# Cross attention in a decoder layer: the row sums of seven batches go through DRAM to 128 rows of 32, are inverted there and come back spread

## The chip, the cores and the metric

One core of a Trainium2 chip runs the whole kernel. The metric is the device time of one execution in microseconds; the median of several runs counts. Five engines work side by side, each through a queue of its own in program order: TensorE (PE in the profile, its weight loads PEld), VectorE (DVE), ScalarE (ACT), GpSimd (POOL) and SyncE (SP, which only issues transfers here). They wait for one another by semaphores.

## What is computed

The reference is a decoder layer over 8 batches of 256 tokens of width 128: self attention with a position bias, cross attention to a context of 1601 rows a batch, a second self attention, a feed-forward block and a mixture of experts. The change lies in the cross attention alone, which is, cut to what matters:

```python
q = _split_heads(x @ qw + qb)          # 16 heads of 8
k = _split_heads(ctx @ kw + kb)
v = _split_heads(ctx @ vw + vb)
scores = jnp.einsum('bqhd,bkhd->bhqk', q, k) / np.sqrt(D // H) + mask
probs = jax.nn.softmax(scores, axis=-1)
out = jnp.einsum('bhqk,bkhd->bqhd', probs, v)
```

The kernel takes the exponentials of the scores less their row maximum, multiplies them by the values with a column of ones beside them, so that every head's product brings its row sum along, and divides at the end, once a batch.

## The kernel before

`phase_cross` (L1244) is the stage in question; it runs from about 210 to 901 us. Its work is cut into 64 units, a unit g being one pair of heads p = 0 to 7 of one batch b. `cross_steps` (L1220) goes through the steps -2 to 64 and hands every engine the same plan, `cross_plan(p)` (L1181), of which each engine runs the kinds that it has an action for. So all engines' queues have the same order, written out by hand. A step of the plan has 13 rounds j, and in them:

- `s`, 13 score tiles of the unit, three rounds ahead: two matmuls on TensorE each (L1360), one exponential on ScalarE (L1478) into one of 8 buffers PT;
- `g`, 16 grains of the unit two steps ahead: a matmul of the scores laid the other way (L1342) into one of 4 banks, and a reduction to the row maximum on VectorE (L1558); `neg` (L1565) joins and negates them;
- `split` (L1635), four small operations on GpSimd that split the negated maxima into three bfloat16 parts, at the very end of a step for the unit two steps ahead; `m` in round 7 of the next step turns them on TensorE (L1391), and ScalarE puts them beside the queries (L1486), where the unit's scores wait for them;
- `v`, three bursts of products with the values (L1380) in rounds 3, 7 and 12, which add up in the bank PO; `o` at the end of the step copies it to a slot of OT (L1494, ScalarE), of which there are ten;
- in rounds 5 and 10 the preparation of the next batch: `T` (p = 0, 1) turns its context (L1405), `K` (p = 2, 3) makes its keys, which GpSimd splits (L1633 to L1661), `V` (p = 4, 5) makes its values (L1583, VectorE).

`c` divides. In round 1 of p = 0 of the next batch TensorE waits for the last copy to OT and runs `head_sums` (L237): 16 float32 matmuls with the selector SEL over the batch's eight slots of OT, of which eight put the values of all 16 heads on 128 rows of 256 queries and eight put each head's row sum on its eight rows (`kind` 0 and 1). Each matmul shows as two records in the trace. VectorE then takes the reciprocal of the sums, 128 x 256 (L1571), and multiplies (L1573) into CAT. The score tiles, `m`, `c`, `T`, `K` and `V` take turns on three banks (`cross_ring` L1237, `take_bank` L1309), so a bank that is held long stops TensorE three turns later.

SyncE meanwhile stores the parts of the keys (L1712) and loads them, eight pairs a batch (L1721, L1722), and the queries every second batch. GpSimd issues no transfer in this stage. The self-attention stages already have the row sums go to DRAM and back, through SyncE (L904 to L927, L1119, L1124).

## Time and profile before

| | us |
|---|---|
| median of 3 runs | 1294.16 |
| lowest and highest run | 1292.65, 1294.98 |
| the profiled execution | 1292.28 |
| its span, first to last instruction | 1290.3 |
| mean granted TensorE clock | 0.92 of full speed |

The rows below are of that execution. A row of the timeline gives the start, the length (with xN, of N instructions merged), the engine, the line, the operation with out<-in, and in brackets how long the engine was idle before and what ended that. A row of windows gives a stretch, its length, and each engine's busy time with the count of instructions; behind them stand the granted clock, the share of the DMA engines' time and GB/s. A busy matmul is not TensorE at its peak, since matmuls are pipelined.

### The profile page before, as it was taken

To read this page: it belongs to the slowest core of one execution; us is meant where nothing else is said; L and a number is where in the kernel's file an instruction comes from. 1 tells how busy PE (TensorE), PEld (TensorE's weight loads), DVE (VectorE), ACT (ScalarE), POOL (GpSimd) and SP (SyncE) were. 2 spreads that over 40 slices of the span, in tenths; PEclk is the share of its full clock that TensorE was granted. 3 is DMA by queue.
4 is the path that set the end of the run, shared out by engine and by line. 5 is a ranking of instruction groups with operands and counts; after the bars stand their busy time and mean duration, and the time that the engine had idled before them with its cause. 6 is when DMAs were issued, how large, how long until landed. Compare 5 with 4: busy or idle time off the path is not lost. (4 is left out here: it accounts for less than half of the span.)

```text
span 1290.3 us, 32652 instructions
## 1 busy us (share of the span) xinstructions
PE 1077.4 (83%) x11660; PEld 576.5 (45%) x11660; DVE 995.1 (77%) x2779; ACT 860.7 (67%) x1764; POOL 406.4 (31%) x832
## 2 busy tenths in 40 slices
PE   5779995699999999999999999997667878539993
PEld 2334443244444444444444444443433445428883
DVE  7458766588889888898888988992777968766664
ACT  3468883087888878877788787785357965425553
POOL 3211213214150230502305023011442515755662
PEclk8689998689999999999999999998878999759997
DMA  6934015523223132231322303100373012301113
GB/s 164 219 70 96 24 29 139 139 65 78 61 55 98 55 79 62 62 95 51 79 62 60 95 27 79 53 5 3 103 148 63 14 46 94 106 13 40 46 48 115
DMA packets 82974, 94.84 MB, mean 73 GB/s; under 512 B 12775, under 2 KB 69039, under 8 KB 82816
## 3 DMA queue, kind: packets, MB, share of 16 engines
q1 hardware_dynamic: 78720, 86.46, 26.7%
q0 software_dynamic: 2496, 5.12, 1.5%
q8 instruction: 96, 1.57, 0.5%
q10 hardware_dynamic: 1600, 1.18, 0.4%
q14 instruction: 62, 0.51, 0.1%
HBM read 66.47 MB, written 27.48 MB: 73 GB/s over the span
## 5 line engine op out<-in xcount | busy, mean ns | idle before, releaser
L1558 DVE TENSOR_REDUCE MG<-bank 128x1 f32<-128x401 f32 (+1 forms) x1024 | 515.4, 566 | 75.2 <-PE bank L1342 73.3
L1478 ACT ACTIVATE PT<-bank 128x512 f32<-128x512 f32 (+1 forms) x624 | 334.7, 597 | 64.2 <-PE bank L1360 63.6
L1360 PE MATMUL bank<-QP,KP 54*128 54x256 bf16 (+1 forms) x1664 | 252.5, 274 | 16.2 <-DVE CAT L1573 4.1
L1342 PE MATMUL bank<-KP,QP 54*128 54x401 bf16 (+1 forms) x1024 | 237.1, 344 | 14.7 <-DMA KP<-ctx_k_parts 9.5
L1380 PE MATMUL bank<-PT,VP 128*9 128x256 f32 (+1 forms) x2688 | 198.2, 368 | 0.8 <-ACT XT L1478 0.8
L1633 POOL TENSOR_TENSOR MP<-MN,ZERO 128x4 bf16<-128x4 f32 x128 | 26.4, 206 | 440.9 <-DVE MN L1565 435.9
L1360 PEld LDWEIGHTS bank<-QP,KP 54*128 54x128 bf16 (+1 forms) x1664 | 110.6, 96 | 108.1 <-ACT PT L1478 24.4
L1342 PEld LDWEIGHTS bank<-KP,QP 54*128 54x128 bf16 x1024 | 75.5, 94 | 125.0 <-DVE MG L1558 93.2
L1004 PE MATMUL bank<-QP,KP 51*128 51x256 bf16 x512 | 97.9, 285 | 39.1 <-DMA QP<-q_parts 12.5
L1478 ACT ACTIVATE XT<-bank 128x512 f32<-128x512 f32 (+1 forms) x208 | 116.2, 599 | 20.3 <-PE bank L1360 19.9
L971 PE MATMUL bank<-KP,QP 51*128 51x256 bf16 x512 | 100.7, 294 | 3.9 <-DVE MG L1099 1.0
L1380 PEld LDWEIGHTS bank<-PT,VP 128*9 128x9 f32 (+1 forms) x2688 | 76.1, 90 | 57.9 <-issue 20.9
L1099 DVE CUSTOM_DVE_ANT_0 JUNK<-bank,UQ 128x256 bf16<-128x256 f32 x256 | 92.4, 420 | 6.7 <-PE bank L971 6.6
L1061 ACT ACTIVATE XT<-bank 128x512 f32<-128x512 f32 x128 | 74.5, 602 | 27.3 <-PE bank L1004 26.6
L1380 PE MATMUL bank<-XT,VP 128*9 128x256 f32 (+1 forms) x896 | 91.9, 369 | 0.0
L1105 DVE TENSOR_REDUCE MN<-bank 128x2 f32<-128x512 f32 x128 | 81.1, 683 | 3.6 <-PE bank L971 1.4
L1150 POOL TENSOR_TENSOR MP<-MN,ZERO 128x8 bf16<-128x8 f32 x128 | 26.4, 206 | 182.1 <-DVE MN L1112 114.1
L1004 PEld LDWEIGHTS bank<-QP,KP 51*128 51x128 bf16 x512 | 33.3, 96 | 110.3 <-issue 68.3
L935 ACT COPY QP<-bank 3x512 bf16<-3x512 bf16 x96 | 55.1, 574 | 36.2 <-PE bank L1038 35.7
L2163 PE MATMUL bank<-WUP,XP 128*128 x234 | 64.1, 409 | 2.4 <-DVE XP L2332 2.4
L1486 ACT COPY QP<-bank 3x256 bf16<-3x256 bf16 x128 | 45.3, 354 | 26.4 <-DMA q_parts<-PT 25.7
L1633 POOL TENSOR_TENSOR KPARTS<-XT,ZERO 128x401 bf16<-128x401 f32 (+1 forms) x56 | 47.6, 851 | 36.7 <-ACT XT L1506 34.5
(283 smaller groups left out, 1870.7 us busy)
## 6 DMA issues: line engine op xcount, KB each, us to landing
KP<-ctx_k_parts SPq DMA_DIRECT2D x128, 100.1 KB
ctx_k_parts<-KPARTS SPq DMA_DIRECT2D x16, 600.4 KB, 5.3
KP<-ctx_k_parts SPq DMA_DIRECT2D x128, 59.4 KB
CN<-in_ctx SPq DMA_DIRECT2D x8, 768.0 KB
RAW<-in_w_gate_up SPq DMA_DIRECT2D x8, 512.0 KB, 3.7
QP<-q_parts SPq DMA_DIRECT2D x20, 192.0 KB
ctx_k_parts<-KPARTS SPq DMA_DIRECT2D x16, 200.1 KB, 5.4
UQ<-bias_table SPq DMA_DIRECT2D x4, 768.0 KB, 8.3
```

The source lines that it names most:

```text
L971: last = nc.tensor.matmul(bank[:, S * qt:S * (qt + 1)], k.QP[rows, p, a:a + 128], k.KP[rows, p, b * S:(b + 1) * S], start=True, stop=True)
L1004: last = nc.tensor.matmul(bank[:, S * t:S * (t + 1)], k.KP[half(s), p, a:a + 128], k.QP[half(s), p, b * S:(b + 1) * S], start=not bias, st ...
L1061: nc.scalar.activation(PT[n % 8], SCORE[n % 3][:, :], ACT.Exp).then_inc(exp_done, 1)
L1099: last = nc.vector.tensor_tensor_reduce(out=JUNK[:, 2 * (n % 2) + q, :], in0=bank[:, S * q:S * (q + 1)], in1=k.UQ[:, 2 * p + s, 128 * q:12 ...
L1105: nc.vector.tensor_reduce(MN[:, u % 3, j, s, :], bank[:, :].rearrange("p (q n) -> p q n", q=QT), AX.X, ALU.max, negate=True).then_inc(grai ...
L1342: nc.tensor.matmul(GRAIN[n % NG][:, 0:w], k.QP[half, p, b * S + 128 * qt:b * S + 128 * (qt + 1)], k.KP[half, p, a:a + w], start=True, stop ...
L1360: return nc.tensor.matmul(bank[0:rows[t], S * at:S * (at + 1)], k.KP[half, p, 128 * t:128 * t + rows[t]], k.QP[half, p, b * S:(b + 1) * S] ...
L1380: last = nc.tensor.matmul(k.PO[32 * c:32 * c + HD + 1, q:q + w], VP[b % 2][0:rows[t], t, 2 * p + s, :], PT[(T * g + n) % NP][0:rows[t], S ...
L1478: nc.scalar.activation(PT[n % NP][0:rows[t], :], bank_of("s", g, t)[0:rows[t], :], ACT.Exp).then_inc(exp_done, 1)
L1558: nc.vector.tensor_reduce(MG[:, g % 4, 2 * s + qt, chunk:chunk + 1], GRAIN[n % NG][:, 0:w], AX.X, ALU.max).then_inc(m_read, 1)
L1633: return nc.gpsimd.tensor_tensor(out, x, ZERO[:, :].broadcast_to(list(x.shape)), ALU.add)
L2163: last = nc.tensor.matmul(bank[j % 2], XP[:, j % 2, a, :], WUP[:, bass.ds(e, 1), b, n0:n0 + FF].rearrange("p a n -> p (a n)"), start=(n == ...
```

## The change

For the batches 0 to 6 the row sums no longer go through TensorE. GpSimd, at the end of every step (`o`), waits for the copy to OT and sends the four rows that hold the sums to DRAM (`take_sums`). At p = 0 of the next batch it waits for all eight and loads the sums as 128 rows of 32, in two halves (`spread_sums`, `x`). At p = 1 VectorE adds the halves and takes the reciprocal of 128 x 32 (`reciprocals`, `r`), and GpSimd sends that to DRAM and loads it back spread over 128 rows of 256 (`return_reciprocals`). At p = 2 TensorE selects the values alone, eight matmuls (`batch_values`, `c`), and VectorE multiplies (`scale`). ScalarE's copy to a slot of OT waits for the slot's transfer too. The last batch is divided as before (`e`).

```diff
--- before.py
+++ after.py
@@ -162,6 +162,7 @@
     k.dYS = dram("expert_rows", [2 * TOK + 128 * SLOT_TILES, D], F32)
     k.dSums = dram("head_sums", [H, S], F32)
     k.dRec = dram("head_reciprocals", [H, S], F32)
+    k.dHalves = dram("half_sums", [PAIRS, 4, S], F32)
     k.dMask = dram("mask_parts", [3, B * NCTX], BF16)
 
 
@@ -234,9 +235,9 @@
     return divmod(g, PAIRS)
 
 
-def head_sums(k, bank, slot_of, b):
-
-    for kind in range(2):
+def head_sums(k, bank, slot_of, b, kinds=(0, 1)):
+
+    for kind in kinds:
         for parity in range(2):
             for j in range(4):
                 last = k.nc.tensor.matmul(bank[32 * j:32 * j + 32, S * kind:S * (kind + 1)], k.SEL[:, kind, parity, :],
@@ -1194,8 +1195,10 @@
             plan.append(("h", T - 1, t // T))
         if j in (5, 10) and rounds:
             plan.append(rounds[j // 10])
-        if j == 1 and p == 0:
-            plan.append(("c", 0, 0))
+        if j == 1 and p < 3:
+            plan.append((("e", "r", "c")[p], 0, 0))
+            if p == 0:
+                plan.append(("x", 0, 0))
         if j in bursts:
             if bursts[j] == 1:
                 plan.append(("m", 0, 1))
@@ -1227,8 +1230,11 @@
             if what in ("T", "K", "V"):
                 if 0 <= b < LAST_BATCH:
                     actions[what](b + 1, i)
-            elif what == "c":
-                if b > 0:
+            elif what in "rcx":
+                if 0 < b < B:
+                    actions[what](b - 1, i)
+            elif what == "e":
+                if b == B:
                     actions[what](b - 1, i)
             elif 0 <= step + ahead < B * PAIRS:
                 actions[what](step + ahead, i)
@@ -1237,7 +1243,7 @@
 def cross_ring():
 
     turns = [(what, 0, i) for what in "TKV" for i in range(4)]
-    cross_steps({what: lambda unit, i, what=what: turns.append((what, unit, i)) for what in "smcTKV"})
+    cross_steps({what: lambda unit, i, what=what: turns.append((what, unit, i)) for what in "smceTKV"})
     return turns
 
 
@@ -1275,6 +1281,7 @@
         MN = k.sb("MN", [128, 4, 4], stack=st)
         MP = k.sb("MP", [128, 4, 4, 3], BF16, stack=st)
         REC = k.sb("REC", [128, S], stack=st)
+        SUMS = k.sb("SUMS", [128, 4, SEGMENT], stack=st)
         ZERO = k.sb("ZERO", [128, 1], stack=st)
         CN = k.sb("CN", [128, T, D], stack=st)
         CT = k.sb("CT", [128, T * 128], stack=st)
@@ -1289,6 +1296,8 @@
         neg_ready, max_split, m_turned, m_rows = sem("neg_ready"), sem("max_split"), sem("m_turned"), sem("m_rows")
         s_ready, exp_done, pv_done = sem("s_ready"), sem("exp_done"), sem("pv_done")
         o_read, sums_turned, rec_done, sums_done = sem("o_read"), sem("sums_turned"), sem("rec_done"), sem("sums_done")
+        sums_out, sums_in, sums_added = sem("sums_out"), sem("sums_in"), sem("sums_added")
+        compact_done, rec_out, rec_in = sem("compact_done"), sem("rec_out"), sem("rec_in")
         qk_in = [sem(f"qk_in{c}") for c in range(4)]
         vp_set, zero_made, psum_cleared = sem("vp_set"), sem("zero_made"), sem("psum_cleared")
         ctx_in, ctx_turned, ctx_t_taken = sem("ctx_in"), sem("ctx_turned"), sem("ctx_t_taken")
@@ -1315,7 +1324,7 @@
                         pe.wait_ge(exp_done, T * a + j + 1)
                     elif old == "m":
                         pe.wait_ge(m_rows, a + 1)
-                    elif old == "c":
+                    elif old in "ce":
                         pe.wait_ge(sums_done, a + 1)
                     elif old == "T":
                         pe.wait_ge(ctx_t_taken, 4 * a + j + 1)
@@ -1392,9 +1401,13 @@
                                                k.IDB[:, :])
                 last.then_inc(m_turned, 1)
 
-            def batch_sums(b, i):
+            def batch_values(b, i):
                 pe.wait_ge(o_read, PAIRS * (b + 1))
-                head_sums(k, take_bank("c", b, i), lambda g: OT[:, g % NO, :], b).then_inc(sums_turned, 1)
+                head_sums(k, take_bank("c", b, i), lambda g: OT[:, g % NO, :], b, (0,)).then_inc(sums_turned, 1)
+
+            def last_values(b, i):
+                pe.wait_ge(o_read, PAIRS * (b + 1))
+                head_sums(k, take_bank("e", b, i), lambda g: OT[:, g % NO, :], b).then_inc(sums_turned, 1)
 
             def turn_context(b, i):
                 if i == 0:
@@ -1463,8 +1476,8 @@
                 make_queries(g)
             for i in range(4):
                 make_values(0, i)
-            cross_steps({"s": scores, "h": last_tile, "g": grain, "v": values, "m": max_rows, "c": batch_sums,
-                         "T": turn_context, "K": make_keys, "V": make_values})
+            cross_steps({"s": scores, "h": last_tile, "g": grain, "v": values, "m": max_rows, "c": batch_values,
+                         "e": last_values, "T": turn_context, "K": make_keys, "V": make_values})
 
         @block.scalar
         def _(act):
@@ -1491,6 +1504,7 @@
                 act.wait_ge(pv_done, NV * (g + 1))
                 if g >= NO:
                     act.wait_ge(sums_turned, (g - NO) // PAIRS + 1)
+                    act.wait_ge(sums_out, 16 * PAIRS * ((g - NO) // PAIRS + 1))
                 nc.scalar.copy(OT[:, g % NO, :], k.PO[:, 0:S]).then_inc(o_read, 1)
 
             def take_turned(b, i):
@@ -1565,11 +1579,26 @@
                 nc.vector.tensor_reduce(MN[:, g % 4, :], MG[:, g % 4, :, :], AX.X, ALU.max,
                                         negate=True).then_inc(neg_ready, 1)
 
-            def divide(b, i):
-                bank = bank_of("c", b, i)
+            def reciprocals(b, i):
+                v.wait_ge(sums_in, 32 * (b + 1))
+                nc.vector.tensor_tensor(SUMS[:, 2, :], SUMS[:, 0, :], SUMS[:, 1, :], ALU.add).then_inc(sums_added, 1)
+                v.wait_ge(sums_added, b + 1)
+                if b > 0:
+                    v.wait_ge(rec_out, 16 * b)
+                nc.vector.reciprocal(SUMS[:, 3, :], SUMS[:, 2, :]).then_inc(compact_done, 1)
+
+            def scale(b, i):
+                v.wait_ge(rec_in, 16 * (b + 1))
                 v.wait_ge(sums_turned, b + 1)
+                nc.vector.tensor_tensor(k.CAT[:, b * S:(b + 1) * S], bank_of("c", b, i)[:, 0:S], REC[:, :],
+                                        ALU.mult).then_inc(sums_done, 1)
+
+            def divide_last(b, i):
+                bank = bank_of("e", b, i)
+                v.wait_ge(sums_turned, b + 1)
+                v.wait_ge(sums_done, b)
                 nc.vector.reciprocal(REC[:, :], bank[:, S:2 * S]).then_inc(rec_done, 1)
-                v.wait_ge(rec_done, b + 1)
+                v.wait_ge(rec_done, 1)
                 nc.vector.tensor_tensor(k.CAT[:, b * S:(b + 1) * S], bank[:, 0:S], REC[:, :],
                                         ALU.mult).then_inc(sums_done, 1)
 
@@ -1622,7 +1651,7 @@
             v.wait_ge(late_in, 48)
             for i in range(4):
                 take_values(0, i)
-            cross_steps({"g": maxima, "neg": negate, "c": divide, "V": take_values})
+            cross_steps({"g": maxima, "neg": negate, "r": reciprocals, "c": scale, "e": divide_last, "V": take_values})
 
         @block.gpsimd
         def _(pl):
@@ -1681,7 +1710,37 @@
             split_first_keys(3)
             split_queries(2)
             split_queries(3)
-            cross_steps({"split": split_maxima, "K": split_keys})
+            def take_sums(g, i):
+                b, p = batch_of(g)
+                if b == LAST_BATCH:
+                    return
+                pl.wait_ge(o_read, g + 1)
+                if p == 0 and b > 0:
+                    pl.wait_ge(sums_in, 32 * b)
+                nc.gpsimd.dma_start(k.dHalves.ap()[p], OT[HD:128:32, g % NO, :]).then_inc(sums_out, 16)
+
+            def spread_sums(b, i):
+                pl.wait_ge(sums_out, 16 * PAIRS * (b + 1))
+                if b > 0:
+                    pl.wait_ge(compact_done, b)
+                for half in range(2):
+                    src = bass.AP(tensor=k.dHalves.ap().tensor, offset=2 * S * half,
+                                  ap=[[4 * S, PAIRS], [SEGMENT, 2 * S // SEGMENT], [1, SEGMENT]])
+                    nc.gpsimd.dma_start(SUMS[:, half, :], src).then_inc(sums_in, 16)
+
+            def return_reciprocals(b, i):
+                pl.wait_ge(compact_done, b + 1)
+                if b > 0:
+                    pl.wait_ge(rec_in, 16 * b)
+                nc.gpsimd.dma_start(compact(k.dRec), SUMS[:, 3, :]).then_inc(rec_out, 16)
+                pl.wait_ge(rec_out, 16 * (b + 1))
+                if b > 0:
+                    pl.wait_ge(sums_done, b)
+                src = bass.AP(tensor=k.dRec.ap().tensor, offset=0, ap=[[S, H], [0, HD], [1, S]])
+                nc.gpsimd.dma_start(REC[:, :], src).then_inc(rec_in, 16)
+
+            cross_steps({"split": split_maxima, "K": split_keys, "o": take_sums, "x": spread_sums,
+                         "r": return_reciprocals})
             pl.wait_ge(late_in, 48)
             pl.wait_ge(y_turned, 4)
             for g in range(4):
```

## Rows read from the trace of the kernel before

**Rows 1.** The page's part 1: busy time, share of the span, instructions.

```profile
PE 1077.4 (83%) x11660; PEld 576.5 (45%) x11660; DVE 995.1 (77%) x2779; ACT 860.7 (67%) x1764; POOL 406.4 (31%) x832
```

**Rows 2.** Windows, copy L1494 to copy: stretch, length, PE, PEld, DVE, ACT, POOL busy.

```profile
420.65:432.83 12.18, 11.18 (x145) 5.33 (x143) 10.57 (x21) 8.82 (x19) 0.82 (x4) 1.00 0.16 50
432.83:442.32 9.49, 9.12 (x110) 4.37 (x108) 8.02 (x17) 8.10 (x18) 0.81 (x4) 1.00 0.13 42
442.32:452.31 9.99, 9.55 (x109) 4.24 (x107) 8.51 (x18) 8.71 (x18) 5.61 (x10) 1.00 0.24 66
...
483.11:491.90 8.79, 8.24 (x105) 3.80 (x103) 8.12 (x18) 7.51 (x17) 0.82 (x4) 1.00 0.20 59
...
822.15:833.49 11.34, 10.50 (x137) 4.64 (x135) 10.22 (x20) 7.75 (x16) 0.81 (x4) 1.00 0.17 51
833.49:842.28 8.79, 8.24 (x105) 3.77 (x103) 8.14 (x18) 7.52 (x17) 0.81 (x4) 1.00 0.08 28
```

**Rows 3.** Timeline at the division of the second batch, p = 0.

```profile
420.65 0.37 ACT L1494 COPY OT<-bank 128x256 f32<-128x256 f32 x1 [0.51 <-PE bank L1380]
...
420.89 0.17 DVE L1565 TENSOR_REDUCE MN<-MG 128x4 f32<-128x16 f32 x1
...
421.05 1.06 DVE L1558 TENSOR_REDUCE MG<-bank 128x1 f32<-128x401 f32 x2
...
421.08 1.93 PE L242 MATMUL bank<-OT,SEL 128*32 128x256 f32 x32
...
422.95 0.35 PE L1342 MATMUL bank<-KP,QP 54*128 54x401 bf16 x2
...
423.08 1.76 DVE L1571 RECIPROCAL REC<-bank 128x256 f32<-128x256 f32 x1 [0.97 <-PE bank L242]
...
423.54 0.60 ACT L1478 ACTIVATE PT<-bank 128x512 f32<-128x512 f32 x1 [1.51 <-PE bank L1360]
...
424.87 0.42 DVE L1573 TENSOR_TENSOR CAT<-bank,REC 128x256 f32<-128x256 f32 x1
...
425.36 0.39 PE L1360 MATMUL bank<-QP,KP 54*128 54x256 bf16 x2 [0.58 <-DVE CAT L1573]
```

**Rows 4.** Timeline of a plain step, from 833.49 us.

```profile
833.89 2.02 DVE L1558 TENSOR_REDUCE MG<-bank 128x1 f32<-128x401 f32 x4
...
834.43 0.11 PEld L1360 LDWEIGHTS bank<-QP,KP 54*128 54x128 bf16 x2 [0.41 <-ACT PT L1478]
...
836.12 2.50 DVE L1558 TENSOR_REDUCE MG<-bank 128x1 f32<-128x401 f32 x5 [0.21 <-PE bank L1342]
```

**Rows 5.** One line's instructions: durations in ns, minimum, median, maximum.

```profile
L1119 DVE RECIPROCAL SUMS<-SUMS x14: 341/348/353, 95.7 to 1050.8; 128x32 f32<-128x32 f32 x14
```

**Rows 6.** GpSimd's own transfers, in the expert stage: durations, landings, one timeline row.

```profile
L2396 POOL DMA_INDIRECT XG<-expert_tokens,G_ROW x39: 952/977/1223, 1150.7 to 1258.5; - x39
...
DMA to landing us min/median/max: 2.4/2.7/3.6
...
1181.44 0.98 POOL L2396 DMA_INDIRECT XG<-expert_tokens,G_ROW  x1 [0.30 <-issue]
```

**Rows 7.** Timeline: last operation of a split on POOL, and L1391 after it.

```profile
413.20 0.21 POOL L1646 TENSOR_TENSOR MP<-MN,MP 128x4 bf16<-128x4 f32 x1
...
415.94 0.23 PE L1391 MATMUL bank<-IDB,MP 128*3 128x128 bf16 x2 [0.19 <-ACT PT L1478]
...
455.52 0.21 POOL L1646 TENSOR_TENSOR MP<-MN,MP 128x4 bf16<-128x4 f32 x1
...
456.94 0.23 PE L1391 MATMUL bank<-IDB,MP 128*3 128x128 bf16 x2 [0.26 <-ACT XT L1506]
...
465.48 0.21 POOL L1646 TENSOR_TENSOR MP<-MN,MP 128x4 bf16<-128x4 f32 x1
...
467.45 0.22 PE L1391 MATMUL bank<-IDB,MP 128*3 128x128 bf16 x2 [0.58 <-DVE VP L1583]
```

**Rows 8.** SyncE's queue: one line's issues in ns; landings of L927.

```profile
L1721 SPq DMA_DIRECT2D KP<-ctx_k_parts x128: 302/1973/2654, 236.4 to 827.2; - x128
...
DMA to landing us min/median/max: 2.3/2.4/4.4
```

## The prediction

> **What bounds the kernel now.** I read the busy time first: TensorE leads with 83% of the span, VectorE follows with 77% [rows 1]. That is an average over stages, so the second view was the cross-attention loop cut into its steps, from one copy of L1494 to the next [rows 2]. A step is one pair of heads of one batch, numbered p = 0 to 7 in a batch. A step without extra work (p = 6) takes 8.79 us, with TensorE busy for 8.24, VectorE for 8.12 and ScalarE for 7.51 of them: no engine has more than a few tenths of a microsecond to spare, and the three wait for each other in turn. Work put into a step therefore lengthens it, and the way to price the change is to compare steps. In the last batch nothing but the division stands between p = 0 (11.34 us) and the plain step after it (8.79 us): the present division costs 2.55 us a batch. The granted clock is 1.00 in all of these steps (the 2.4 GHz level), so no part of the sum is the clock's.
>
> The third view is the timeline at that place [rows 3]. TensorE spends from 421.08 to 422.95 us, 1.87 us, on the 16 selection matmuls (32 records). VectorE, done with two reductions at 422.11, waits until 423.08, divides (1.76 us) and multiplies (0.42 us). TensorE then waits 0.58 us for the bank of the product, and ScalarE is left without scores for 1.51 us.
>
> The fourth view is the same place in a plain step [rows 4]: TensorE waits 0.41 us for an exponential before the seventh score tile, and VectorE waits 0.21 us after its fourth reduction. These two gaps can swallow a small insert.
>
> **The change part by part.** *Removed from p = 0, seven times.* In the last batch it is worth 2.55 us by the subtraction above. In the six others p = 0 also turns two tiles of context; without the division it cannot be expected below p = 1 (9.49 us), which turns a full group and a short one, so at most 12.18 - 9.49 = 2.69 us goes. If p = 1's surplus of 0.70 us were 1.25 groups, a full one would cost 0.56, p = 0 would stay at 8.79 + 1.12 = 9.91, and 2.27 us would go. I take 2.55, since one price for the division then explains both kinds of p = 0. Seven times 2.55 is 17.85 us; the ends are 6 x 2.27 + 2.55 = 16.2 and 6 x 2.69 + 2.55 = 18.7.
>
> *Added to p = 2: eight matmuls and the multiplication.* Half of the 1.87 us is 0.93 us on TensorE. They sit ahead of the 0.41 us wait for the exponential, which goes on meanwhile, so 0.52 us remains. VectorE's 0.42 us multiplication follows its two reductions (about 1.06 us) and ends before TensorE's next grains are there; the bank is back before the third ring turn asks for it, so the 0.58 us wait goes too. The data of the wait on `o_read` have been there for two steps. Cost 7 x 0.52 = 3.6 us. Ends: 0.4 a batch (a little more absorbed), and half of today's 2.55, that is 1.28, if the insert costs in proportion: 2.8 and 9.0 us.
>
> *Added to p = 1: an addition and a reciprocal of 128 x 32.* The reciprocal of that shape takes 0.34 us in the self-attention stage; for the addition the nearest row is the 128 x 16 reduction, 0.17 us [rows 3, 5]. Together with the handover about 0.5 us on VectorE, of which the 0.21 us wait after the fourth reduction covers a part: 0.29 us a batch, 2.0 us in all. Ends 0 and 0.55: 0 and 3.9 us. The addition alone has bounds of nothing and 0.34 us, the reciprocal of its own size; I take the reduction's, the nearer in work.
>
> *GpSimd's queue.* In each of 56 steps a transfer of four rows of 1 KB now stands ahead of the four small operations that split the maxima, and it waits for the copy L1494. That copy ends at 421.02, the negated maxima are ready at 421.06 [rows 3], so the wait adds nothing; the issue does. No plain transfer is issued by GpSimd in this trace. Its indirect ones hold it 0.98 us, and 0.30 us passes to the next [rows 6]: 1.28 us, which I take, since that is its own queue. The lower bound is nothing (issued while it idles), the upper the longest issue of SyncE's loads of keys, 2.65 us [rows 8]. Behind it wait the split, then TensorE's turning of the maxima (L1391), then the scores of the next pair. The time from the end of the split to L1391 [rows 7] is 415.94 - 413.41 = 2.53 us in a plain step, 456.94 - 455.73 = 1.21 us in p = 3 and 467.45 - 465.69 = 1.76 us in p = 4, because GpSimd is still splitting keys at the ends of p = 2 and p = 3. So 1.28 us is hidden everywhere but in p = 3, where 0.07 us, with the signal some 0.15 us, is left: 7 x 0.15 = 1.0 us.
>
> *The chain of transfers.* The copy L1494 of p = 7 starts at 420.65 and ends at 421.02 [rows 3]. The row transfer issued then lands about 2.7 us later (the indirect median, [rows 6]), at 423.7; two spreading transfers are issued at 423.7 and 425.0 and land by 427.7. The addition on VectorE comes after the first two reductions of p = 1, 1.4 us behind the next copy (833.49 to 834.9 in [rows 2, 4]), at 420.65 + 9.63 + 1.4 = 431.7: 4.0 us to spare. From there 0.5 for addition and reciprocal, 2.7 for the way out and 2.7 for the way back give 437.6; the multiplication in p = 2 asks one step later, at 431.7 + 9.78 = 441.5: 3.9 us to spare. Even with 4.4 us for each landing, the longest of the same broadcast on SyncE's queue [rows 8], the addition's inputs land at 431.1 and the multiplication's at 441.0, just in time. I cost the waits at nothing; if the cover is gone, each microsecond late is a microsecond on VectorE in seven batches, 7 us. ScalarE's new wait, for the rows to have left their slot, is for transfers two steps old. `take_sums` of p = 0 also waits for the spread rows (427.7), three microseconds before its turn. The six semaphores and the unchanged last batch cost nothing.
>
> **The sum.** -17.85 + 3.6 + 2.0 + 1.0 = -11.2 us. The profiled execution took 1292.28 us (span 1290.3 us) and would come to 1281.1; the median of the runs stands 1.88 us above it, and by the same difference comes to 1283.0 us. The best ends together give -18.7 + 2.8 = -15.9 us (1278.3), the worst with GpSimd's 1.28 us -16.2 + 9.0 + 3.9 + 1.0 = -2.3 us (1291.9).
>
> **Rivals.** *The insert keeps its price.* What costs in p = 0 may be the interruption itself. For it: the 2.55 us are more than TensorE's 1.87. Against it: 0.58 us of them is the wait for the product's bank [rows 3], which goes. It gives -17.85 + 9.0 + 3.9 + 1.0 = -4.0 us, 1290.2 us.
>
> *The rows arrive late.* The transfers become the bound: VectorE waits at the addition or the multiplication. The addition is late once a landing takes more than (431.7 - 421.0 - 1.3) / 2 = 4.7 us, the multiplication beyond (441.5 - 432.2) / 2 = 4.65 us. At 5.1 us each the two waits are 0.8 + 0.9 = 1.7 us a batch, 11.9 us in all, and nothing of the gain is left: 1294.9 us. Against it stand medians of 2.4 to 2.7 us.
>
> *GpSimd is held, and the maxima come late.* This one ends slower, in the split queue at the head of p = 3 and p = 4. With an issue of x us these steps wait (x - 1.21) + (x - 1.76); without the 1.0 us of the sum -12.2 us has to be eaten, 1.74 us a batch, so it decides from x = 2.36 us. At SyncE's 2.65 us it is 2.33 us a batch, and the 16 plain steps p = 6 and p = 7 add 0.12 each: 7 x 2.33 + 16 x 0.12 = 18.2 us, so 1294.2 - 12.2 + 18.2 = 1300.2 us. For it: SyncE does take that long beside the loads of keys. Against it: GpSimd's own rows keep within 1.22 us.
>
> The Trainium skill, page "DMA: Bandwidth & Descriptors", section "Issuing engine by pattern", gives plain loads and stores to SyncE and only indirect ones to GpSimd, which speaks against this change; its page "SBUF — State Buffer", section "Who interferes with whom", says how this rival could come about: a transfer from GpSimd's queue cannot get its descriptors while VectorE runs an operation in a two-port mode. The same section exempts reductions, which are most of VectorE's work in this loop. By that rule GpSimd is not held, and no row here shows a plain GpSimd transfer beside reductions, so the rival keeps the smaller chance.
>
> *It doesn't do what it says* would show as unchanged steps; the work moved is visible in the code, and I give it nothing of its own.
>
> **How the numbers follow.** The forecast (a gain of 6 to 16 us) has 0.66, the insert that keeps its price 0.16, late rows 0.08, GpSimd held 0.10. A difference of 0.2% (2.6 us) is what a measurement of this kernel can tell from none. The first two cases are faster but for the far end of the second, and a little of the late rows: 0.83. Same is 0.08, from late rows and that end, slower 0.09, nearly all GpSimd's. The range, 1278 to 1292 us, holds the forecast with its bounds and the second case; both slow cases are left out, some 0.15.
>
> **What would show it.** Steps p = 0 near 9.63, p = 1 near 9.8, p = 2 near 10.5 and p = 3 near 10.15 us, with p = 4 to 7 as now; 16 records of L242 in p = 2; no VectorE wait at the new lines; GpSimd's transfers at about 1.0 us each. I am wrong if L1391 waits for GpSimd, if the addition waits for a transfer, or if p = 2 grows by more than 1 us.

## The result, and the profile after

| | before | after |
|---|---|---|
| median, us | 1294.57 (4 runs) | 1316.77 (4 runs) |
| lowest and highest run | 1292.65, 1295.32 | 1312.73, 1317.65 |
| profiled execution, its span | 1292.28, 1290.3 | 1317.65, 1315.4 |
| first copy L1494 / L1508 to the last in the loop | 272.80 to 894.17: 621.37 | 273.97 to 915.75: 641.78 |
| mean granted clock | 0.920 | 0.909 |

The ratio is 1.017 (95% interval 1.0149 to 1.0190): slower by 22 us, where 11 us less was forecast and the range ended at 1292. In the loop 20.4 us were lost. Line numbers moved: the copy to OT is L1508 now, the reduction L1572 (L1558), the score tiles L1369 (L1360), the selection L243 (L242), `m` L1400 (L1391). New are L1584 (addition), L1588 (reciprocal of 128 x 32), L1593 (product), and GpSimd's transfers L1720 (rows out), L1729 (rows spread), L1735 (reciprocals out) and L1740 (reciprocals back).

The page's busy times of the changed kernel:

```profile
PE 1086.7 (83%) x11548; PEld 579.4 (44%) x11548; DVE 985.1 (75%) x2786; ACT 861.7 (66%) x1764; POOL 455.2 (35%) x916
```

Beside [rows 1], VectorE has 10 us less work, as intended, and TensorE shows 9 us more although 112 records of it are gone: a first sign of a lower clock. Next the windows of the changed kernel, batch 2, from copy to copy (p = 0, 1, 2, 3 and 6), then p = 2 alone in three pieces; columns as in [rows 2]:

```profile
426.46:436.09 9.63, 9.27 (x113) 4.50 (x111) 8.47 (x19) 8.47 (x18) 2.66 (x7) 1.00 0.19 58
436.09:445.59 9.50, 9.13 (x110) 4.47 (x108) 8.42 (x19) 8.12 (x19) 2.56 (x7) 1.00 0.16 51
445.59:460.65 15.06, 12.32 (x125) 5.03 (x123) 8.83 (x19) 9.06 (x18) 6.21 (x11) 0.89 0.19 53
460.65:470.64 9.99, 9.55 (x109) 4.24 (x107) 8.34 (x17) 8.71 (x18) 8.52 (x14) 1.00 0.01 3
491.44:500.22 8.78, 8.22 (x105) 3.83 (x105) 8.11 (x18) 7.51 (x16) 1.40 (x5) 1.00 0.23 69
...
445.59:449.00 3.41, 3.19 (x46) 1.26 (x42) 1.23 (x3) 2.46 (x5) 1.41 (x5) 1.00 0.80 222
449.00:452.40 3.40, 0.94 (x6) 0.38 (x6) 1.51 (x4) 0.60 (x1) 0.00 (x0) 1.00 0.05 13
452.40:455.90 3.50, 3.50 (x25) 1.51 (x28) 2.37 (x5) 2.29 (x5) 1.21 (x2) 0.52 0.00 0
```

p = 0 fell from 12.18 us [rows 2] to 9.63, the number of the forecast. p = 1 and p = 3 are as before. The whole loss of this batch is in p = 2: 15.06 us where some 10.5 was forecast. Its middle 3.4 us have TensorE busy for 0.94, and in the 3.5 us after that its granted clock is 0.52, the 1.2 GHz level nearly throughout. Over the batches, p = 2 took 14.52, 15.06, 17.55, 16.62, 17.60, 11.39 and, in the last, 10.46 us; p = 1 took 12.16 in batch 1, where the granted clock fell too, and 9.5 to 10.2 after. The waits of the changed kernel (280 to 930 us: engine, line, what it waited for, us in total, times, longest) name what ends last:

```profile
DVE CAT L1593 <- DMA REC<-head_reciprocals: 25.7, 7, 5.7
...
DVE SUMS L1584 <- DMA SUMS<-half_sums: 4.6, 6, 1.5
...
POOL REC L1740 <- DMA head_reciprocals<-SUMS: 34.2, 7, 5.7
POOL half_sums L1720 <- DMA SUMS<-half_sums: 30.8, 6, 6.1
...
PE bank L1369 <- DVE CAT L1593: 16.8, 6, 4.4
```

VectorE waits at the product for the reciprocals to come back, in all seven batches (3.35, 3.85, 5.67, 4.14, 5.43, 1.41, 1.88 us), and TensorE behind it for the product's bank. One whole chain, batch 2, in the timeline of the changed kernel (POOL, DVE, SP, PE; columns as in [rows 3]):

```profile
427.12 0.58 POOL L1720 DMA_DIRECT2D half_sums<-OT  x1 [7.12 <-ACT OT L1508]
...
432.19 1.25 POOL L1729 DMA_DIRECT2D SUMS<-half_sums  x2 [3.41 <-DMA half_sums<-OT]
438.15 0.57 POOL L1720 DMA_DIRECT2D half_sums<-OT  x1 [4.71 <-DMA SUMS<-half_sums]
...
440.09 0.61 POOL L1735 DMA_DIRECT2D head_reciprocals<-SUMS  x1 [0.29 <-issue]
444.97 0.55 POOL L1740 DMA_DIRECT2D REC<-head_reciprocals  x1 [4.27 <-DMA head_reciprocals<-SUMS]
...
437.64 0.19 DVE L1584 TENSOR_TENSOR SUMS<-SUMS 128x32 f32<-128x32 f32 x1
437.86 0.35 DVE L1588 RECIPROCAL SUMS<-SUMS 128x32 f32<-128x32 f32 x1
...
450.88 0.42 DVE L1593 TENSOR_TENSOR CAT<-bank,REC 128x256 f32<-128x256 f32 x1 [3.85 <-DMA REC<-head_reciprocals]
...
443.27 0.40 SPq L1758 DMA_DIRECT2D CN<-in_ctx  x1
...
451.37 0.39 PE L1369 MATMUL bank<-QP,KP 54*128 54x256 bf16 x2 [2.59 <-DVE CAT L1593]
```

From the addition (437.64) to the product (450.88) 13.24 us pass; the forecast had 5.9. The product was asked for at 447.03, 9.4 us after the addition. The 7.3 us too many are 1.9 in which GpSimd holds the reciprocals back (it waited with p = 0's rows for the spread rows until 438.15, then did the split), 2.2 on the way out (440.09 to 444.97 is 4.9, not 2.7) and 3.2 on the way back (444.97 to 450.88 is 5.9, not 2.7). All seven, in ns and us, from the views of the three lines of the changed kernel:

```profile
L1729 POOL DMA_DIRECT2D SUMS<-half_sums x14: 612/628/637, 347.5 to 850.1; - x14
...
DMA to landing us min/median/max: 2.3/3.8/6.1
...
L1735 POOL DMA_DIRECT2D head_reciprocals<-SUMS x7: 589/601/623, 356.5 to 855.8; - x7
...
DMA to landing us min/median/max: 4.6/4.8/6.0
...
L1740 POOL DMA_DIRECT2D REC<-head_reciprocals x7: 548/548/551, 362.5 to 860.7; - x7
...
DMA to landing us min/median/max: 3.2/5.9/6.3
```

The issues are short, 0.55 to 0.63 us at the medians: GpSimd is not held. It is the landing that is long, the time from the issue until the last part of the transfer has arrived. Why, the packet records of the changed kernel show, here those of the last batch (start of the first packet to end of the last, count):

```text
reciprocals out, 1024 B   857.00-857.21: 15 packets    859.75-859.80: 1 packet
reciprocals back, 4096 B  861.95-862.47: 30 packets    864.68-865.01: 2 packets
SyncE's keys, 3202 B      855.10-864.68: 73 packets (of a longer stream, cut at 855), median 131 ns
```

Of 16 equal shares fifteen are there 1.4 to 1.8 us after the start of the issue (855.83 and 860.69), and the last comes some 2.5 us later. The last two packets of the way back start at 864.68, when the stream of key rows ends. That stream is 73 x 131 ns = 9.56 us of packets in 9.58 us: one after the other, as from one DMA engine, long after SyncE's last issue at 850.8. The late share of the way out runs in the one pause of that stream (859.76 to 859.80 us), with 37 of its packets still to come. So a late share does not wait until the stream is over: in both transfers here it waits for about 20 rows of keys, 2.6 and 2.4 us. The stream is the load of 19 rows (L1722 before, L1781 now): 59.4 KB, 19 packets of 131 ns, 2.5 us for each of two per pair of heads.

The Trainium skill, page "DMA: Bandwidth & Descriptors", section "Why a DMA increments its semaphore by 16 and not by 1", says that the transfer's slowest dimension decides over how many engines it is spread (the largest count up to 16 that divides it), and that it counts as landed only when the last of them has finished. By that rule 19 rows go through a single engine, and the packets above agree: 131 ns apart, none side by side.

### The profile page after: what moved, and what is told of

It is laid out like the page before. It is cut to its first block and busy times, and to the rows that moved or that the text cites. A ratio compares the mean times of both kernels' runs of the same rounds, so it can differ in the third digit from the quotient of the medians.

```text
span 1315.4 us, 32557 instructions
## 1 busy us (share of the span) xinstructions
PE 1086.7 (83%) x11548; PEld 579.4 (44%) x11548; DVE 985.1 (75%) x2786; ACT 861.7 (66%) x1764; POOL 455.2 (35%) x916
## 5 line engine op out<-in xcount | busy, mean ns | idle before, releaser
L1572 DVE TENSOR_REDUCE MG<-bank 128x1 f32<-128x401 f32 (+1 forms) x1024 | 514.7, 566 | 81.7 <-PE bank L1351 79.8
L1369 PE MATMUL bank<-QP,KP 54*128 54x256 bf16 (+1 forms) x1664 | 256.8, 277 | 29.0 <-DVE CAT L1593 16.8
L1351 PE MATMUL bank<-KP,QP 54*128 54x401 bf16 (+1 forms) x1024 | 240.2, 347 | 17.2 <-DMA KP<-ctx_k_parts 9.4
L1389 PE MATMUL bank<-PT,VP 128*9 128x256 f32 (+1 forms) x2688 | 200.9, 372 | 0.8 <-ACT XT L1491 0.8
L1369 PEld LDWEIGHTS bank<-QP,KP 54*128 54x128 bf16 (+1 forms) x1664 | 112.4, 97 | 121.8 <-ACT PT L1491 24.5
L1720 POOL DMA_DIRECT2D half_sums<-OT x56 | 32.9, 587 | 262.0 <-ACT OT L1508 231.2
## 6 DMA issues: line engine op xcount, KB each, us to landing
KP<-ctx_k_parts SPq DMA_DIRECT2D x128, 59.4 KB
```

Of the source, the lines that this page charges most:

```text
L1351: nc.tensor.matmul(GRAIN[n % NG][:, 0:w], k.QP[half, p, b * S + 128 * qt:b * S + 128 * (qt + 1)], k.KP[half, p, a:a + w], start=True, stop ...
L1369: return nc.tensor.matmul(bank[0:rows[t], S * at:S * (at + 1)], k.KP[half, p, 128 * t:128 * t + rows[t]], k.QP[half, p, b * S:(b + 1) * S] ...
L1389: last = nc.tensor.matmul(k.PO[32 * c:32 * c + HD + 1, q:q + w], VP[b % 2][0:rows[t], t, 2 * p + s, :], PT[(T * g + n) % NP][0:rows[t], S ...
L1572: nc.vector.tensor_reduce(MG[:, g % 4, 2 * s + qt, chunk:chunk + 1], GRAIN[n % NG][:, 0:w], AX.X, ALU.max).then_inc(m_read, 1)
```

## The experiments

**Theory A**: the 19-row loads keep one DMA engine busy, and every transfer that passes over all 16 waits for it. The rivals: GpSimd's queue itself is slow (theory B in the expectations), or its many small transfers disturb the loop; the chain is too long wherever it runs. **Theory C** came later, from the context load at 443.27 above.

**The 19 rows cut into 16 and 3**, in the changed kernel (LOADS counts three loads accordingly):

```diff
-                    sp.dma_start(k.KP[r + 4 * HD:r + 6 * HD + 3, p, 0:N],
-                                 dC[b, s, 2 * HD:4 * HD + 3, p, :]).then_inc(kp_in[p], 16)
+                    sp.dma_start(k.KP[r + 4 * HD:r + 6 * HD, p, 0:N],
+                                 dC[b, s, 2 * HD:4 * HD, p, :]).then_inc(kp_in[p], 16)
+                    sp.dma_start(k.KP[r + 6 * HD:r + 6 * HD + 3, p, 0:N],
+                                 dC[b, s, 4 * HD:4 * HD + 3, p, :]).then_inc(kp_in[p], 16)
```

> The changed kernel with one edit outside it: SyncE's load of 19 rows of keys is cut into 16 and 3 rows, so that its bytes spread over the DMA engines. Theory A (one DMA engine is busy with these 19-row loads, and every GpSimd transfer leaves a sixteenth on it that lands last): the reciprocals land in 2.7 us or less on the way out and back (4.8 and 5.9 us now), VectorE waits under 1 us in all for REC (25.7 us now), p = 2 takes about 10.5 us, and the time is 1283 us, within 4 us. Theory B (transfers from GpSimd's queue are that slow by themselves): landings stay at 4.8 and 5.9 us and the time at 1313 to 1318 us.

Measured: 1270.73 us (1268.59 to 1275.07), ratio 0.9806 (0.9783 to 0.9829). Its windows of p = 1 and p = 2 in batch 2:

```profile
425.12:434.61 9.49, 9.12 (x110) 4.38 (x108) 8.32 (x19) 8.11 (x18) 2.57 (x7) 1.00 0.16 43
434.61:445.21 10.60, 10.29 (x125) 4.50 (x123) 8.93 (x19) 8.82 (x19) 6.22 (x11) 1.00 0.20 57
```

The lines of its transfers out and back, and of the first of SyncE's loads of keys:

```profile
L1735 POOL DMA_DIRECT2D head_reciprocals<-SUMS x7: 584/601/623, 349.4 to 816.9; - x7
...
DMA to landing us min/median/max: 1.7/1.7/2.2
...
L1740 POOL DMA_DIRECT2D REC<-head_reciprocals x7: 547/548/551, 351.9 to 819.4; - x7
...
DMA to landing us min/median/max: 2.2/2.4/2.4
...
L1780 SPq DMA_DIRECT2D KP<-ctx_k_parts x128: 302/303/1459, 238.1 to 804.3; - x128
```

VectorE waits at neither new line any more, the clock stays at 1.00, p = 0, 1, 2 take 9.63, 9.50 and 10.60 us in every one of the six middle batches, 8.78, 8.78 and 9.38 in the last; the loop takes 605.25 us. SyncE's issues, 1973 ns in [rows 8], take 303: that long median had been the backlog of the one engine. This version beats both kernels.

**The same cut in the kernel before.** The diff is the same.

> The kernel before with the same cut of the 19-row loads. Nothing in it waits for the keys after the start, so by both theories the time stays at 1294.6 us, within 3 us; by theory A SyncE's issues of key loads no longer take 2 to 2.65 us. It tells whether e1's gain, if there is one, comes from the loads alone.

Measured: 1289.47 us (10 runs), ratio 0.9960 (0.9937 to 0.9982); expected was no change within 3, so it missed by 5. The steps are as before (p = 0 at 12.17 us), but the first copy comes at 269.97 us instead of 272.80. TensorE's one wait for the first batch's keys is shorter (225 to 275 us; the kernel before, then this one):

```profile
PE bank L1342 <- DMA KP<-ctx_k_parts: 9.5, 1, 9.5
...
PE bank L1342 <- DMA KP<-ctx_k_parts: 4.6, 1, 4.6
```

The expectation had left the start of the stage out. The seven traces with a load of 19 or 17 rows have the first copy at 272.80 to 275.95 us, the three with even loads at 269.24 to 269.97, so the start can hold all of the 5 us. Inside the loop, the slow engine cost the kernel before nothing; the change made it matter. Between this kernel and the first experiment lie 18.7 us by the medians and 15.4 by the profiled executions (1290.51 and 1275.07). 15.0 of these are in the loop: 13.6 by the steps, and 1.4 because one p = 0 with the division took 13.57 us here.

**17 and 2 rows instead of 16 and 3**, as many loads and bytes:

```diff
-                    sp.dma_start(k.KP[r + 4 * HD:r + 6 * HD + 3, p, 0:N],
-                                 dC[b, s, 2 * HD:4 * HD + 3, p, :]).then_inc(kp_in[p], 16)
+                    sp.dma_start(k.KP[r + 4 * HD:r + 6 * HD + 1, p, 0:N],
+                                 dC[b, s, 2 * HD:4 * HD + 1, p, :]).then_inc(kp_in[p], 16)
+                    sp.dma_start(k.KP[r + 6 * HD + 1:r + 6 * HD + 3, p, 0:N],
+                                 dC[b, s, 4 * HD + 1:4 * HD + 3, p, :]).then_inc(kp_in[p], 16)
```

> A control for e1: the same number of transfers, but the 19 rows are cut into 17 and 2, so that 17 of them should still go through one engine. Theory A: SyncE's issues stay near 2 us in the median, the reciprocals land in 4 us or more each, and the time is 1305 us or more. If cutting the load in two were what helped in e1, whatever the rows, this one would come to about 1271 us too.

Measured: 1306.32 us (1301.68 to 1313.39), ratio 1.0095 (1.0059 to 1.0132). Lines of the way out and of SyncE's loads of keys:

```profile
L1735 POOL DMA_DIRECT2D head_reciprocals<-SUMS x7: 587/603/626, 358.5 to 851.5; - x7
...
DMA to landing us min/median/max: 4.6/4.7/5.3
...
L1780 SPq DMA_DIRECT2D KP<-ctx_k_parts x128: 307/311/1953, 241.0 to 845.2; - x128
...
L1783 SPq DMA_DIRECT2D KP<-ctx_k_parts x128: 229/1732/2424, 241.7 to 845.9; - x128
```

The way out lands late again, so it is the divisor of the row count that decides, not the smaller load. SyncE's issues were expected near 2 us. At L1780 they are short at the median, and one line later they are long: the load of two rows, which now comes right behind the 17, takes 1732 ns. A long issue shows the backlog where the next load meets it. The way back landed in 4.4 us at the median (2.3 to 5.9), earlier than in the changed kernel; VectorE waited 11.9 us for it in all instead of 25.7, which goes with the 10 us between the two times.

**Rows out alone**, in the kernel before: GpSimd's 56 transfers of rows as in the change, into a scratch that nothing reads, and ScalarE's wait for them.

```diff
+                nc.gpsimd.dma_start(k.dHalves.ap()[g], OT[HD:128:32, g % NO, :]).then_inc(sums_out, 16)
...
-            cross_steps({"split": split_maxima, "K": split_keys})
+            cross_steps({"split": split_maxima, "K": split_keys, "o": take_sums})
```

> The kernel before with GpSimd's 56 row transfers added and nothing made of them; the division stays as it was. The rival of the held queue makes this slower than 1297 us; with an issue of 0.59 us, as the changed kernel's trace shows, nothing waits behind it and the time stays at 1294.6 us, within 2 us.

Measured: 1293.43 us (10 runs), ratio 0.9994 (0.9976 to 1.0012). The steps are unchanged. The line of the transfers:

```profile
L1694 POOL DMA_DIRECT2D half_sums<-OT x56: 574/575/824, 275.6 to 824.8; - x56
```

GpSimd's 56 transfers of rows cost nothing by themselves.

**The reciprocals out and back by ScalarE**, in rounds 4 and 12 of p = 1, in the changed kernel:

```diff
+            def give_reciprocals(b, i):
+                act.wait_ge(compact_done, b + 1)
...
+                nc.scalar.dma_start(compact(k.dRec), SUMS[:, 3, :]).then_inc(rec_out, 16)
+
+            def place_reciprocals(b, i):
+                act.wait_ge(rec_out, 16 * (b + 1))
...
+                nc.scalar.dma_start(REC[:, :], src).then_inc(rec_in, 16)
```

> The changed kernel with the 19-row loads as they are; the reciprocals' way out and back is issued by ScalarE (rounds 4 and 12 of p = 1) instead of GpSimd. If the busy engine delays whatever passes it (theory A as it stands after e1), both transfers still land last on that engine: about 4 to 6 us each, VectorE still waits 2 us or more a batch for REC, and the time stays above 1305 us. If only GpSimd's queue loses against SyncE's on that engine (B in a weaker form), the broadcast lands in about 2.5 us as in the self attention, VectorE hardly waits and the time falls below 1292 us.

Measured: 1315.41 us (1308.76 to 1316.25), ratio 1.0156 (1.011 to 1.0201). The line of the way out:

```profile
L1516 ACTq DMA_DIRECT2D head_reciprocals<-SUMS x7: 331/331/356, 355.4 to 858.1; - x7
...
DMA to landing us min/median/max: 5.1/5.3/7.2
```

The way back landed in 4.1 to 7.2 us. Another queue, the same lateness: whose queue it is does not matter here.

**The product one step later**, at p = 3, with an eleventh slot of OT and two scratch buffers, so that nothing is waited for in its place:

```diff
-            plan.append((("e", "r", "c")[p], 0, 0))
+            plan.append(({0: "e", 1: "r", 3: "c"}[p], 0, 0))
...
-    NP, NO = 8, 10
+    NP, NO = 8, 11
```

> The changed kernel with more time for the transfers and no faster ones: the values are selected and multiplied at p = 3 instead of p = 2 (eleven slots of OT instead of ten), and the row sums in DRAM have two buffers, so that GpSimd doesn't wait for the spread rows ahead of the next split. By both theories landings stay as late as now, but only the addition at p = 1 still waits (4.6 us in all now), and the time comes to the sum of the prediction plus that, 1283 to 1289 us. If it stays above 1294 us, other terms of the sum were wrong too: the insert at p = 2 or the reciprocal at p = 1.

Measured: 1284.66 us (1278.75 to 1285.14), ratio 0.9904 (0.9873 to 0.9936). Landings stay at 4.7 to 6.1 us on the way out, and on the way back:

```profile
L1740 POOL DMA_DIRECT2D REC<-head_reciprocals x7: 547/548/551, 362.1 to 832.6; - x7
...
DMA to landing us min/median/max: 4.6/5.8/6.4
```

Yet VectorE waits nowhere for the reciprocals; p = 2 takes 9.99 us and p = 3 10.59. The insert costs the same 0.60 us there. What is left against the first experiment in the traces is p = 1 at 9.57 to 10.78 us, where the addition still waits (5.3 us in all), two longer plain steps (0.9 us), and the start, 5.2 us later.

**The context load held back.** In the chain above, SyncE issues 800 KB of the context two batches ahead at 443.27, as soon as p = 1 has turned the last one, and the way back is issued 1.7 us later. In batches 6 and 7, which have no such load, VectorE waits only 1.41 and 1.88 us. Theory C: A makes the way out late, and the way back then falls into this load. In the changed kernel:

```diff
                 if b + 2 < B:
+                    if b > 0:
+                        sp.wait_ge(sums_done, b)
                     load_context(b + 2)
```

> The changed kernel, the key loads as they are; only SyncE's load of the context two batches ahead (800 KB, issued near the end of p = 1) waits until the product in p = 2 is made. Theory A (the loads of 19 keys alone delay the transfers): the broadcast of the reciprocals still lands in 4.8 to 6 us in batches 1 to 5, p = 2 stays at 14.5 to 17.6 us, time 1310 to 1317 us. Theory C (loads of keys make the way out 3 us late, and the broadcast then falls into the load of the context, which fills all DMA engines): VectorE's waits in batches 1 to 5 fall from 3.4 to 5.7 us to the 1.4 to 1.9 us of batches 6 and 7, p = 2 falls to about 11.5 us, TensorE's granted clock stays up after it, and the time falls by some 28.4 - 5 x 0.95 = 23.6 us to about 1293 us.

Measured: 1303.06 us (1300.65 to 1305.21), ratio 1.0071 (1.0046 to 1.0096): between the two. VectorE's waits at the product, from its timeline, batches 1 to 6:

```profile
368.12 0.42 DVE L1593 TENSOR_TENSOR CAT<-bank,REC 128x256 f32<-128x256 f32 x1 [3.82 <-DMA REC<-head_reciprocals]
...
448.35 0.42 DVE L1593 TENSOR_TENSOR CAT<-bank,REC 128x256 f32<-128x256 f32 x1 [1.37 <-DMA REC<-head_reciprocals]
...
530.32 0.42 DVE L1593 TENSOR_TENSOR CAT<-bank,REC 128x256 f32<-128x256 f32 x1 [4.41 <-DMA REC<-head_reciprocals]
...
611.60 0.42 DVE L1593 TENSOR_TENSOR CAT<-bank,REC 128x256 f32<-128x256 f32 x1 [1.03 <-DMA REC<-head_reciprocals]
```

Batches 2 and 4 do as theory C says (p = 2 at 11.36 and 11.02 us). The odd ones stay (15.04, 16.65, 16.71 us), and neither theory had them apart. In odd batches SyncE also loads queries, right behind the keys (six issues of L218 hold it from 350.08 to 362.44). By the packet records, the queries' share on the one engine takes turns with the key rows: the last 74 packets of keys of batch 1 take 11.9 us where 74 x 131 ns is 9.7, and their stream reaches 366.29, 2.0 us after VectorE asked. The packets of batch 3 of this kernel show it: 30 of the 32 shares of the way back at 526.49 to 527.09, the last two at 529.38 to 529.75, and the keys' 3202 B packets until 529.25. There A alone is enough. In batch 7 of this kernel p = 1 took 11.75 us, at a granted clock of 0.76, after a wait of 1.32 us at the addition.

**The way back held until the context load, with even loads**: the first experiment, with GpSimd's L1740 moved to round 10 of p = 1 behind the same event that SyncE waits for.

```diff
+            def place_reciprocals(b, i):
+                pl.wait_ge(rec_out, 16 * (b + 1))
+                pl.wait_ge(ctx_turned, 4 * min(b + 3, B))
```

> The kernel with the loads of keys cut into 16 and 3 rows, with the broadcast of the reciprocals held on GpSimd until the context is turned, the point at which SyncE issues the next load of 800 KB; the way out stays where it was. Theory A (only the loads of 19 rows delay): the broadcast lands in 2.4 us, 2.3 + 1.5 - 2.4 = 1.4 us before VectorE asks for it, all steps stay as in the kernel with even loads, 1270.7 us within 2. Theory C (the load of the context does it as well): it lands in 4.5 to 6 us in batches 1 to 5, VectorE waits 1 to 2.5 us there, p = 2 is 11.5 to 13 us in these five and stays at 10.6 and 9.4 in batches 6 and 7, time 1276 to 1283 us.

Measured: 1279.18 us (1278.23 to 1280.41), ratio 0.9896 (0.9865 to 0.9927), as theory C expected. The line of the way back, and the window of p = 2 in batch 2:

```profile
L1745 POOL DMA_DIRECT2D REC<-head_reciprocals x7: 547/548/551, 354.4 to 826.5; - x7
...
DMA to landing us min/median/max: 2.2/5.2/5.5
```

```profile
435.95:448.11 12.16, 10.81 (x125) 4.59 (x123) 8.75 (x19) 8.96 (x18) 6.21 (x11) 1.00 0.24 66
```

p = 2 is 11.76 to 12.25 us in batches 1 to 5 and 10.60 and 9.39 in the two without a context load. VectorE waits 10.3 us in all, the five steps are longer by 7.25, and the clock stays at 1.00. The hold itself is not what delays: in batch 6 the way back is issued as late after the addition as in batch 2 (6.34 us in both), and it lands in 2.4 us where batch 2 has 5.4.

## Why the prediction was wrong, step by step

**What bounds the loop**, and the way to price work by steps, held.

**Removed from p = 0**: 2.55 us a batch forecast, 12.17 - 9.63 = 2.54 measured; in the last batch 11.34 - 8.79. Right.

**Added to p = 2**: 0.52 us forecast; with even loads it is 10.60 - 9.99 = 0.61, in the last batch 9.38 - 8.78 = 0.60. Right to 0.1. The insert that keeps its price (1.28) did not come.

**Added to p = 1**: 0.29 forecast, nothing measured (9.50 before and after). The addition takes 0.18 to 0.19 us and the reciprocal 0.35, as the rows said, but there were more waits to swallow them: in the first experiment VectorE still waits 0.35 us before these reductions and 0.76 after.

**GpSimd's queue**: 0.15 forecast, nothing measured. The issue was mis-sized: a plain transfer holds GpSimd 0.58 us, not the 1.28 us of an indirect one. So the rival that ends slower failed too: L1400 waits for GpSimd 1.5 us in all. (That rival counted 16 plain steps p = 6 and p = 7; only 14 of them have a transfer, 0.24 us less.) The Trainium skill's "SBUF — State Buffer", "Who interferes with whom", exempts reductions, and here GpSimd's issues beside them (0.82 us at the longest) agree.

With even loads, these four give -17.8 + 4.2 = -13.6 us of steps, against the forecast's -11.2.

**The chain of transfers, costed at nothing: this step failed.** Two of the prediction's own signs of being wrong came: the addition waited for a transfer, and p = 2 grew by 5.1 us in batch 2. Four readings in the step were wrong. First, the landing of 2.7 us [rows 6] came from the expert stage, and 2.4 to 4.4 us [rows 8] from the self-attention, neither beside the loads of keys; in the place itself the reciprocals take 4.8 us out and 5.9 back at the medians. Second, the reason stood in [rows 8] and was read only as a price of issuing: a line whose issue takes 302 ns at best and 1973 at the median is waiting for something, and that was the one engine that is behind. Third, the order of GpSimd's queue: the reciprocals out stand behind p = 0's rows and split. The spread rows should have been there three microseconds before p = 0's rows had their turn; these went out only at 438.15, 1.7 us after the end of their copy at 436.46. So the reciprocals were held back 1.9 us; 0.7 us of that stays with even loads, where the rows are in time. Fourth, the context load was in the trace of before too (440.01 us, in p = 1), and the forecast's landing at 437.6 was never set against it.

**The rival "rows arrive late"** is what came; it had 0.08, and its landings of 5.1 us were close to those measured, but it let them cost 11.9 us. With GpSimd's 1.9 us and the context load ahead of the way back, VectorE waited 25.7 + 4.6 us. The excess of the steps over those with even loads is 30.3 us in p = 2 and 5.2 in p = 1. -13.6 + 35.4 = 21.8 us agrees with the loop's +20.4 when one p = 0 of 13.57 us in the trace of before (its granted clock was 0.50 from 587.9 to 591.3) is put back, 1.4 us.

**"Each microsecond late is a microsecond"** holds only roughly. Where the clock stayed up, a wait cost 0.6 us less than itself (2.06 us of wait, 1.45 of step, at the mean of the last experiment's five; 0.6 and 0.8 less in batches 6 and 7 of the changed kernel). Where the clock fell (behind the waits of 3.4 us and more at the product, and behind one of 1.46 us at the addition) the step grew by more than the wait.

**How much of the price is whose** is settled in part. All of it goes with even loads, so A is necessary everywhere. Batches 2 and 4 need the context load besides: without it their waits fall from 3.85 and 4.14 to 1.37 and 1.03 us. What the falls of the clock cost alone was not run; it is an estimate below.

## What to carry to other kernels

Before a chain of small transfers is costed, look at what the other queues move at the same moment in that very stage, and read an issue that takes several times its own minimum as an engine that is behind. A load whose row count has no large divisor up to 16 (19 and 17 rows here) delayed the small transfers that pass over all engines, long after its issue. It cost the loop nothing until something short started to wait, so cut such a load into 16 and a rest. And set each planned landing against the big loads around it in the trace of before: a transfer that is 3 us late may meet one that it would have escaped.

## What the runs showed of the hardware that was not expected

- A plain transfer issued by GpSimd held it 0.55 to 0.63 us at the medians and landed in 1.7 us (16 KB out) and 2.4 us (128 KB broadcast back) when the DMA engines were free; behind the loads of 19 rows in 4.6 to 6.0 and 3.2 to 6.3 us. ScalarE's queue (0.33 us for an issue out, 0.55 back) was hit the same: 5.1 to 7.2 and 4.1 to 7.2 us.
- One DMA engine moved rows of 3202 B in 131 ns each, 24 GB/s; its backlog lasted up to 14 us after SyncE's last issue (850.8 to 864.7 us). A share of another queue's transfer was let through after about 20 such rows (last batch of the changed kernel), with the backlog still there.
- TensorE's granted clock fell to the 1.2 GHz level for 3.4 us (batches 1 and 2) and 6.8 us (3 to 5) behind VectorE's waits of 3.4 to 5.7 us at the product; TensorE had been nearly idle before (0.94 of 3.4 us busy in batch 2). Behind waits of 1.0 to 2.3 us at the product (batches 6 and 7, the even batches with the context load held back, and the last experiment) it stayed at 2.4 GHz. The length of the wait alone does not tell, though. In p = 1 of batch 1 the clock fell for 3.4 us behind a wait of 1.46 us at the addition, and with the product one step later it stayed up in the same step behind 1.39 us (windows of the changed kernel, then of that one):

```profile
351.44:363.60 12.16, 10.56 (x110) 4.83 (x108) 8.58 (x20) 8.36 (x19) 2.57 (x7) 0.86 0.29 82
...
352.25:363.01 10.76, 9.21 (x110) 4.40 (x108) 8.41 (x19) 8.35 (x18) 2.57 (x7) 1.00 0.29 83
```

An estimate of the price: the step's excess less the wait was 0.6 us with the short fall and 1.3 to 1.9 us with the long one, against -0.6 without, so 1.2 and 1.9 to 2.5 us each, some 9 us of the 30 in p = 2.
